# A Flamingo layer: the two largest experts searched in the logits, the softmax on GpSimd beside VectorE's chain, separate buffers for the last token tiles, the last row normalised on VectorE

## The reference

```python
x = x + tanh(g_xattn) * xattn(layernorm(x), ctx, token_ids, Wq, Wkv, Wo)      # window of 4 keys per token, 16 heads
x = x + tanh(g_ffn)   * moe(layernorm(x), gate_w, w1, b1, w2, b2)

def moe(x, gate_w, w1, b1, w2, b2):                    # 8 experts, 2 for each token, hidden size 1024
    gate_logits = einsum('bsh,eh->bse', x, gate_w)
    gate_probs = softmax(gate_logits, axis=-1)
    top_v, top_i = top_k(gate_probs, 2)
    comb_w = einsum('bsk,bske->bse', top_v, one_hot(top_i, 8))
    out = 0
    for e in range(8):
        h = silu(x @ w1[e] + b1[e]);  out += (h @ w2[e] + b2[e]) * comb_w[..., e:e + 1]
```

## Time and profile before

| | |
|---|---|
| median of 3 runs | 356.49 us (355.97 to 356.59) |
| the profiled execution's own time | 356.92 us |
| its span | 355.1 us |
| PE busy in the span | 322.9 us, 91% |
| the page's chain that ended last | PE 63%, DVE 20% |
| DVE, ACT, POOL busy | 76%, 49%, 58% |
| HBM read and written | 42.29 MB, 10.17 MB |

### The profile page before, as it was taken

The page is one execution under the profiler, slowest core; times in us unless marked ns, Lnnn a source line. Parts: engine busy times, 40 slices in busy tenths (PEclk is TensorE's granted clock), DMA queues, the critical chain, the costliest instruction groups (busy, mean ns, idle before and its releaser), DMA issues.

```text
span 355.1 us, 11441 instructions
## 1 busy us (share of the span) xinstructions
PE 322.9 (91%) x3486; PEld 266.3 (75%) x3486; DVE 269.9 (76%) x638; ACT 174.1 (49%) x490; POOL 205.9 (58%) x223
## 2 busy tenths in 40 slices
PE   8789989999977989999999999999999999999930
PEld 7457778888877877888888888888888887778710
DVE  5649999999978887778877788777887875656520
ACT  2452255565455456656555565654656543253400
POOL 3476889996752071566656757477473764662330
PEclk9999999999999899999999999999999999999985
DMA  7799999998999421232323323232332323241210
GB/s 250 246 362 412 405 420 404 404 351 327 344 384 391 119 64 34 32 60 37 56 38 64 46 47 48 50 61 38 57 48 48 53 42 61 35 68 26 33 18 13
DMA packets 31406, 53.23 MB, mean 150 GB/s; under 512 B 4834, under 2 KB 25554, under 8 KB 29300
## 3 DMA queue, kind: packets, MB, share of 16 engines
q0 software_dynamic: 9408, 26.63, 29.5%
q1 hardware_dynamic: 15972, 22.44, 17.6%
q10 hardware_dynamic: 5968, 3.39, 3.1%
HBM read 42.29 MB, written 10.17 MB: 148 GB/s over the span
## 4 chain that ended last, share of the span: by engine, by line
PE 63%; DVE 20%; issue 5%; DMA 5%; ACT 2%; POOL 2%; DVEq 0%; ACTq 0%; POOLq 0%
PE ps L1090 28%; PE ps L1104 16%; PE ps L1107 8%; DVE ps L1270 5%; DVE sel L1266 2%; PE ps L1118 2%; PE ps L1112 2%; DMA sel<-near_rows,win_near 2%; DVE w_parts L1266 2%; DMA tokens_split<-xsplit 2%; DVE xs L1302 1%; PE ps L1111 1%; PE ps L1106 1%; DMA near_rows<-w_parts 1%; DVE ps L1274 1%
## 5 line engine op out<-in xcount | busy, mean ns | idle before, releaser
L1090 PE MATMUL ps<-sel,w_parts 128*128 128x128 f16 x1776 | 141.3, 219 | 1.0 <-issue 1.0
L1090 PEld LDWEIGHTS ps<-sel,w_parts 128*128 x1776 | 119.3, 98 | 26.0 <-issue 1.8
L823 ACT ACTIVATE sel<-ps,b1T 128x128 f32<-128x128 f32 x296 | 84.3, 368 | 91.4 <-PE ps L1090 89.4
L596 POOL DMA_INDIRECT out<-sel x37 | 63.1, 1706 | 85.9 <-DVE sel L1540 74.0
L1104 PE MATMUL ps<-w_parts,sel 128*128 x259 | 96.3, 379 | 0.4
L1107 PE MATMUL ps<-w_parts,sel 128*128 x259 | 70.6, 273 | 0.0
L588 POOL DMA_INDIRECT sel<-tokens_split,sel x37 | 43.7, 1180 | 18.9 <-DVE sel L1463 12.6
L1495 DVE SCALAR_TENSOR_TENSOR sel<-sel 128x512 f16<-128x512 f32 x74 | 51.3, 694 | 2.5
L1481 DVE SCALAR_TENSOR_TENSOR w_parts<-w_parts (+1 forms) x32 | 39.0, 1220 | 8.4 <-issue 7.2
L1493 DVE TENSOR_SCALAR sel<-sel 128x512 f16<-128x512 f32 x74 | 33.2, 448 | 10.4 <-ACT sel L823 10.0
L583 POOL TENSOR_TENSOR sel<-sel 128x1 f32<-128x1 f32 x37 | 39.8, 1076 | 1.9 <-PE ps L1118 1.9
(11 more groups left out here) (221 smaller groups left out, 462.1 us busy)
## 6 DMA issues: line engine op xcount, KB each, us to landing
w_parts<-in_L_ffn_w SPq DMA_DIRECT2D x16, 1024.0 KB
out<-xs SPq DMA_DIRECT2D x16, 128.0 KB
tokens_split<-xsplit ACTq DMA_DIRECT2D x16, 128.0 KB, 6.2
xs<-in_x ACTq DMA_DIRECT2D x2, 512.0 KB, 7.1
xs<-in_x SPq DMA_DIRECT2D x2, 512.0 KB, 7.7
near_rows<-w_parts SPq DMA_DIRECT2D x4, 256.0 KB, 9.2
sel<-tokens_split,sel POOLq DMA_INDIRECT x37
out<-sel POOLq DMA_INDIRECT x37
```

Source lines behind the costliest of these rows:

```text
L596: pool.indirect_dma_start(out_rows, bass.IndirectOffsetOnAxis(slot_row[:, at(q - 1)], 0), y_sb[(k + 3) % 4], None, compute_op=ALU.add).the ...
L823: act.activation(h32[n][:, c * P:c * P + P], ps_h[n][:, c * P:c * P + P], ACT.Silu, bias=biases[:, c:c + 1], scale=1.0 / (X_SCALE * W_SCALE))\
L1090: mm = pe.matmul(ps_h[n][:, c * P:c * P + P], w, xx, start=(i == 0), stop=(i == len(products) - 1))
```

## The change

```diff
+        late_x2T = sel0[:, 1024:1536].rearrange("p (n k c) -> p n k c", n=2, k=KC)
+        late_split = sel1[:, 1024:1792].bitcast(F16).rearrange("p (n c) -> p n c", n=3)
...
         def turned_at(u):
-            return ps_x2T[:, 0:256] if u < LATE else ps_late[0][:, 0:256]
+            return ps_x2T[:, 0:256] if u < LATE else ps[:, 2 * (u % 2), 0:256]
         def logits_at(u):
-            return ps_logit[:, 0:E] if u < LATE else ps_late[1][:, 0:E]
+            return ps_logit[:, 0:E] if u < LATE or u % 2 else ps[:, 1, 0:E]
+        def x2T_at(u):
+            return x2T[:, :, :] if u < LATE else late_x2T[:, u % 2, :, :]
+        def split_at(u):
+            return xsplit[:, u % 3, :] if u < T - 3 else late_split[:, u - T + 3, :]
@@ SyncE @@
+            sp.wait_ge(s["comb_ok"], 4)
+            sp.dma_start(xd.rearrange("(t p) d -> p t d", p=P)[:, :, D:XD], r_comb[:, :, :]).then_inc(s["comb_in"], 16)
             sp.wait_ge(s["b2_zeroed"], 1)
@@ GpSimd, norms, behind the power @@
+                if u == T - 1:
+                    return
@@ GpSimd, behind remainder(T - 1) @@
+            pool.wait_ge(s["rt"], RT_TOP)
+            pool.tensor_tensor(r_tmp[:, :, :], logit[:, :, :], r_m8[:, :, 0:1].to_broadcast([P, T, E]), ALU.subtract)\
+                .then_inc(s["shifts_ok"], 1)
+            pool.wait_ge(s["rt_exp"], 1)
+            pool.wait_ge(s["rt"], RT_CUM)
+            pool.tensor_scalar(r_p[:, :, :], r_ex[:, :, :], gate2[:, 0:1], None, ALU.mult).then_inc(s["comb_ok"], 1)
+            pool.tensor_tensor(r_p[:, :, :], r_p[:, :, :], r_m16[:, :, :], ALU.mult).then_inc(s["comb_ok"], 1)
+            pool.wait_ge(s["rt"], RT_INVERSE)
+            pool.tensor_tensor(r_comb[:, :, :], r_p[:, :, :],
+                               r_rs[:, :].rearrange("p (t o) -> p t o", o=1).to_broadcast([P, T, E]), ALU.mult)\
+                .then_inc(s["comb_ok"], 2)
@@ ScalarE @@
-                wait(act, f"xd_out{u % 3}", 16 * (u // 3))
-                act.activation(xsplit[:, u % 3, 0:D], x2[:, u % 2, :], ACT.Copy).then_inc(s["x2hi_ok"], 1)
+                if u < T - 3:
+                    wait(act, f"xd_out{u % 3}", 16 * (u // 3))
+                act.activation(split_at(u)[:, 0:D], x2[:, u % 2, :], ACT.Copy).then_inc(s["x2hi_ok"], 1)
...
-                wait(act, "logit_ps", u)
+                wait(act, "logit_ps", u if u < LATE else u - 1)
...
-            act.wait_ge(s["rt"], RT_COMB)
-            act.dma_start(xd.rearrange("(t p) d -> p t d", p=P)[:, :, D:XD], r_comb[:, :, :]).then_inc(s["comb_in"], 16)
@@ TensorE @@
-            spin(48)
+            spin(36)
             pe.wait_ge(s["rt"], RT_CUM)
@@ VectorE @@
+            def top_two(some):
+                dve.wait_ge(s["logit_ok"], some.stop)
                 for t in range(some.start, some.stop):
-                    ins = v.max(r_m8[:, t, :], r_p[:, t, :])
+                    ins = v.max(r_m8[:, t, :], logit[:, t, :])
                 link(ins)
                 for t in range(some.start, some.stop):
-                    ins = v.max_index(r_i8[:, t, :], r_m8[:, t, :], r_p[:, t, :])
+                    ins = v.max_index(r_i8[:, t, :], r_m8[:, t, :], logit[:, t, :])
                 link(ins)
+            def chosen(some):
+                link(v.tensor_tensor(r_oh[:, :, some, :], found, numbers, ALU.is_equal))
                 link(v.tensor_tensor(r_m16[:, some, :], r_oh[:, 0, some, :], r_oh[:, 1, some, :], ALU.add))
+            def last_x():
+                dve.wait_ge(s["rstd2_ok"], norm_call(T - 1) + 1)
+                v.tensor_scalar(x2[:, 1, :], xs[:, T - 1, :], mv2[:, c:c + 1, 0], rstd2[:, c:c + 1], ALU.subtract, ALU.mult)\
+                    .then_inc(s["x2_last"], 1)
+            early, late = slice(0, T - 5), slice(T - 5, T)
+            top_two(early)
             residual(T - 1)
             second_moments(T - 1)
-            choose(slice(0, LATE), 0)
-            shifted_logits(slice(LATE, T))
-            choose(slice(LATE, T), 1)
+            chosen(early)
+            last_x()
+            top_two(late)
+            chosen(late)
...
-            link(v.scalar_tensor_tensor(out=r_comb[:, :, :], in0=r_p[:, :, :], scalar=gate2[:, 0:1], in1=r_m16[:, :, :],
-                                        op0=ALU.mult, op1=ALU.mult))
+            dve.wait_ge(s["rt_exp"], 1)
+            link(v.tensor_reduce(r_sum[:, :], r_ex[:, :, :], AX_X, ALU.add))
+            link(v.reciprocal(r_rs[:, :], r_sum[:, :]))
```

More of the change, by code:

```diff
@@ L753, in _ @@
             first_half(T - 4)
+            second_x(T - 3)
             token_out(T - 5)
             attended(T - 1)
+            second_turned(T - 4)
             logits_kept(T - 5)
[L757 to L758 removed]
+            second_turned(T - 3)
             first_half(T - 3)
+            second_x(T - 2)
+            logits_kept(T - 4)
+            logits_kept(T - 3)
             token_out(T - 4)
[L761 to L765 removed]
+            first_half(T - 2)
+            second_turned(T - 2)
             token_out(T - 3)
[L767 to L769 removed]
             logits_kept(T - 2)
+            first_half(T - 1)
             second_turned(T - 1)
             logits_kept(T - 1)
[L773 to L779 removed]
+            token_out(T - 2)
+            token_out(T - 1)
+            act.wait_ge(s["shifts_ok"], 1)
+            act.activation(r_ex[:, :, :], r_tmp[:, :, :], ACT.Exp).then_inc(s["rt_exp"], 1)
             act.activation(var2[:, 0:1], half[:, 0:1], ACT.Silu).then_inc(s["unused"], 1)
[L781 to L782 removed]
             act.wait_ge(s["row_ps"], 1)
@@ L943, in second_turn @@
             def second_turn(u):
-                pe.wait_ge(s["x2_ok"], u + 1)
+                if u < T - 1:
+                    pe.wait_ge(s["x2_ok"], u + 1)
+                else:
+                    pe.wait_ge(s["x2_last"], 1)
                 if u < LATE:
@@ L961, in logits @@
                 elif u > LATE:
-                    pe.wait_ge(s["logit_ok"], u)
+                    pe.wait_ge(s["logit_ok"], u - 1)
                 for c in range(KC):
-                    mm = pe.matmul(logits_at(u), x2T[:, c, :], gateT[:, c, :], start=(c == 0), stop=(c == KC - 1))
+                    mm = pe.matmul(logits_at(u), x2T_at(u)[:, c, :], gateT[:, c, :], start=(c == 0), stop=(c == KC - 1))
                 mm.then_inc(s["logit_ps"], 1)
@@ L1336, in _ @@
             experts = iota[:, 0:E]
-            def shifted_logits(some):
+            def top_two(some):
                 dve.wait_ge(s["logit_ok"], some.stop)
-                link(v.tensor_reduce(r_mx[:, some], logit[:, some, :], AX_X, ALU.max))
-                link(v.tensor_tensor(r_tmp[:, some, :], logit[:, some, :], by_expert(r_mx[:, some]), ALU.subtract))
-            def choose(some, part):
-                n = some.stop - some.start
-                dve.wait_ge(s["rt_exp"], part + 1)
-                link(v.tensor_reduce(r_sum[:, some], r_ex[:, some, :], AX_X, ALU.add))
-                link(v.reciprocal(r_rs[:, some], r_sum[:, some]))
-                link(v.tensor_tensor(r_p[:, some, :], r_ex[:, some, :], by_expert(r_rs[:, some]), ALU.mult))
@@ L1358, in choose @@
-                for a in range(2):
-                    ins = v.tensor_tensor(r_oh[:, a, some, :], r_i2[:, some, a:a + 1].to_broadcast([P, n, E]),
-                                          spread_mid(experts, n), ALU.is_equal)
-                link(ins)
-                link(v.tensor_tensor(r_m16[:, some, :], r_oh[:, 0, some, :], r_oh[:, 1, some, :], ALU.add))
-            shifted_logits(slice(0, LATE))
-            assert done[0] == RT_SHIFT
+            def chosen(some):
+                n = some.stop - some.start
+                found = r_i8[:, some, 0:2].rearrange("p t (a o) -> p a t o", o=1).to_broadcast([P, 2, n, E])
+                numbers = experts.rearrange("p (a t e) -> p a t e", a=1, t=1).to_broadcast([P, 2, n, E])
+                link(v.tensor_tensor(r_oh[:, :, some, :], found, numbers, ALU.is_equal))
+                link(v.tensor_tensor(r_m16[:, some, :], r_oh[:, 0, some, :], r_oh[:, 1, some, :], ALU.add))
@@ L1375, in _ @@
             assert done[0] == RT_CUM
[L1376 to L1378 removed]
+            dve.wait_ge(s["rt_exp"], 1)
+            link(v.tensor_reduce(r_sum[:, :], r_ex[:, :, :], AX_X, ALU.add))
+            link(v.reciprocal(r_rs[:, :], r_sum[:, :]))
+            assert done[0] == RT_INVERSE
             dve.wait_ge(s["rt_ps"], 1)
```

62 lines of the change are left out of this document (26 added, 36 removed).

## The result

| | before | changed |
|---|---|---|
| median of 20 runs, us | 357.16 (355.87 to 359.01) | 354.74 (353.52 to 356.44) |
| span of the profiled execution, us | 355.1 | 352.0 |
| PE, DVE in the chain that ended last | 63%, 20% | 65%, 17% |

The ratio is 0.9932 [0.9916, 0.9949]: 2.42 us faster. Forecast were 354.3 us (353.1 to 356.2) and a gain of 2.2. The kernel before came out 0.7 us higher in these 20 runs than in the three shown first, so gain and ratio are the better comparison.

What follows compares the result with a forecast made beforehand. TensorE's expert products were taken to bound, their start set by VectorE's split and the first gather; gather 1.8 us earlier plus 0.4 after the turn gave 2.2: 356.92 to 354.7, less 0.43 for the median, 354.3 us (353.1 to 356.2).

Steps and rivals of the forecast that it cites:

- The chain of DVE, 2.8 us: VectorE's routing up to the slots: 1.4 + 1.7 - 0.1 - 0.2 = 2.8 us sooner, between 2.2 and 3.4.
- That keeps them off this path and brings nothing more: End of attention: the last four tiles avoid the shared x2T, where PE waited 1.53 us; no further gain claimed.
- The gather waits for the pieces: GpSimd's first gather: bound by 2048 short pieces landing at 121.7, not slots at 120.3; starts 122.1, 1.8 us earlier.
- the sooner issue: Pieces issued 2 us sooner gain nothing behind SP's weights; on ACT's queue they would land near 119 to 120.
- The product: PE's first expert product: at 125.95 instead of 128.19, including 0.4 us less between turn and product.
- DVE beside GpSimd, 0.2 us: VectorE's routing operations slowed by GpSimd work alongside: 0.2 us in all, between 0 and 0.9.
- Rival 2: TensorE's clock falls at the experts' start, costing 1.7 us: gain 0.5, 356.0 us (355.2 to 356.5); chance 0.15.
- Rival 1: The pieces don't hold the first gather, so VectorE's chain binds: 353.7 us, down to 353.1; chance 0.15.
- rival 3: SP's transfer of the pieces starts only once its queue is empty: gather 1.8 us later, 358.3 us; chance 0.05.

Runs made afterwards that it cites:

- second profile of before: The kernel before run again with no edit, beside the kernel before: 356.94 us, ratio 0.9993.
- the few pieces: Changed kernel, but 128 pieces of 512 bytes sent to a tensor nobody reads, instead of the 2048 short pieces: 353.97 us, ratio 0.991 to the kernel before.
- the second profile: The changed kernel run again with no edit: 354.8 us, ratio 0.9925 to the kernel before.
- the pieces on ACT's queue: Changed kernel with the 2048 short pieces issued on ScalarE's queue instead of SP's, run twice: 353.87 and 353.66 us, ratios 0.9895 and 0.9896 to the kernel before.
- the last row on ACT: Changed kernel with tile 15 normalised on ScalarE like the other tiles, instead of on VectorE: 354.53 us, ratio 0.993 to the kernel before.
- the search: Alone: changed routing behind the kernel before's attention end; 356.47 us with 48 spins, 355.78 us with 24.
- the buffers: Alone: the kernel before's routing with the changed kernel's buffers and ACT and PE orders, tile 15 on ACT: 356.42 us, ratio 0.9975 to the kernel before.

## Why the prediction was right, and where it was off

- **The chain of DVE, 2.8 us.** Slots done at 21.2 to 21.3 behind the mark for 24.10: 2.8 to 2.9. The parts: 1.36 to the late search (1.4 predicted); 1.58 from there to the scan (3.62 to 2.04; 1.7 predicted, because the mark for 128x40 took 0.43 beside GpSimd's subtraction, where 128x32 had taken 0.29); 0.12 more to the count (0.1). Against the second profile of before the same chain is 4.5 shorter.
- **"That keeps them off this path and brings nothing more"**, said of the shared x2T, is the statement that failed. The wait that goes with it had a low clock behind it in three of four profiles, where the late part began 0.6 to 1.7 us later than in the first profile of before. I had one profile of before, read its 1.53 us as harmless, and was right for that execution only.
- **The gather waits for the pieces.** Shown by its releaser, by the few pieces, and by the sooner landing and gather with the other queue. Landing was put at 121.7 on before's times, mark + 22.7, and came at 22.2 to 22.5; the gather was put at 23.1 and came at 23.1 to 23.4. Two misses of half a microsecond cancel in the first profile: the landing came 0.5 sooner than put, and the gather 0.9 behind it instead of 0.4. The issue, put at 111.3 or mark + 12.3, came at 12.9.
- **Why the sooner issue brings nothing.** The prediction laid it on SP's queue; it holds on ACT's as well. In the thirteen profiles with 2048 pieces they were issued between mark + 12.8 and 16.0, on either queue, and landed between 21.9 and 22.5. Where they land thus hardly depends on the issue. Most of them go as the weights end: on SP's queue 778 packets under 512 bytes in 116 to 117 and 920 in 117 to 118, on ACT's 169 packets and 1255 in the same microseconds of its first profile. The other queue was worth 0.2 to 0.6 us and not the 2 that were named. That the weights' transfer sets the end fits all of this; no run takes the weights away.
- **The product.** Put at mark + 26.9; it stands at 27.41, 28.92 and 28.44. The 0.4 us between turn and product did not go (1.35 us as before): 0.40 of issue and ten spins lie there and not DVE. The rest is the gather's 0.8 to 0.9 us behind the split, foreseen by no term, its start 0.2 to 0.35 later, and in the second profile 0.46 us of spins at the low clock between turn and product.
- **DVE beside GpSimd, 0.2 us.** `L1388` took 0.69 us, 0.55 of it beside the remainder at 103.52, for the 0.3 to 0.48 assumed. From scan to slots nothing is lost: 10.83 us for 10.70 before, of which 0.12 are the sum and the reciprocal.
- **Rival 2, the clock,** came true as an event and not as a price. In the second profile and in two with the pieces on ACT's queue the clock fell in the experts, which the prediction had named as a sign of being wrong, and the first 18 products took 0.8 us longer each time. But of the 1.7 us that the rival charged nothing can be told later on: the turn of the fourth tile stands 9.89, 10.44 and 9.98 us behind the first product in these three, and 10.01 to 10.44 in the other eleven. What stays is 0.4 to 0.6 us ahead of the product, between turn and product. Before has low stretches there too: in its second profile from 123 to 127 us, in the 72 spins, which took 5.81 us and kept PE from rows that were there (turn 3.53 us behind the gather's start, 2.93 in the first profile). So the fall costs some executions of either kernel about half a microsecond, and is no price of the change alone.
- **Rival 1** (pieces don't hold) and **rival 3** (SP's transfer taken up late) fell: SP waited for the pieces 2.8 us, until 120.0.

That the total of 2.2 agrees with the measured 2.42 is in part luck. The product came 0.5 to 2 us later than worked out, and against that the time of before held up to 2 us of low clock and what follows from it in part of its executions, which its first profile did not show. How many these are can be estimated from the mean granted clocks, 0.978 in the first profile of before and 0.969 in the second. Of the 68 runs of before that have such a figure and count in a ratio, 38 lie at 0.973 or below, with a median of 357.6 us, and 30 above, with 356.5. Against runs like the first profile the change is then worth about 1.7 us, and against the others about 2.9. The mean also holds the clock at the end of the program, so this fits the account and doesn't prove it.

Open: how the gain divides between the search and the buffers, since alone the one met the low clock and the other DVE's old routing; why DVE's copy stands 1.4 to 1.6 us behind the turn's start, for 0.4, in one profile each of the last row on ACT and of the pieces on ACT's queue; and whether the course (72 spins at full or at low clock) can be chosen.

## What to carry to other kernels

Count marks from a common event ahead of the change, and take a second profile of the kernel before where a difference under 1% is in question: here one profile hid a wait with a low clock behind it. When a chain is shortened by 3 us, look at everything else that its last consumer waits for; the largest remaining one, here 2048 pieces of 32 bytes at the end of the weights' transfer, becomes the price. Padding work on TensorE in front of a wait is tied to the length of that wait and to the clock: with the shortened search 48 spins at the low clock took 5.28 us and cost VectorE 1.71 us of waiting. 24 at the low clock (2.72 us) and 36 at full clock (2.17 us) cost nothing, and 48 at full clock, 2.84 us before, would by that figure still have ended as the changed kernel's scan did.

## What the runs showed of the hardware

- A gather of 128 rows by GpSimd took 1.10 us started 0.1 to 0.3 us ahead of VectorE's split of fp16 weights (1.23 us), and 2.02 and 1.88 us started 0.18 and 0.33 behind it; the later gathers took mostly 0.95 to 1.04 us, and 1.57 to 2.02 where they started inside the first half of a split.
- 2048 pieces of 32 bytes, issued at mark + 12.8 to 13.1 beside the weights, took 9.1 to 9.7 us to land on either queue, and 8.3 as 128 pieces of 512 bytes; issued 1.5 to 3 us later they took 7.6 to 6.1 and landed at the same place.
- The first gather starts 0.83 to 0.93 us behind the landing that releases it. An 8 KB transfer issued behind 2048 pieces kept SyncE's queue for 5.67 us, and for 0.25 us behind 128 pieces.
- Ahead of the gate product 1.53 us of TensorE idle had full clock behind them and 1.65, 1.70 and 1.87 the low one; ahead of the first turn 1.74 us had full clock and 1.53, 1.58 and 3.01 the low one. The length of the gap alone doesn't tell. A fall at the start of the experts made the first 18 products 0.8 us longer, and ten microseconds later nothing of it could be told from the other profiles.
